# First edge stage of a four-layer graph network: gathered rows held raw in 25 slots, 28 steps ahead

## The reference, cut to what matters

```
edge_index = jnp.stack([src, dst])
# layer 0
row, col = (edge_index[0], edge_index[1])          # row = src, col = dst
msg = x[col] * edge_embed                          # 25000 x 256
agg = segment_sum(msg, row, num_segments=50000)
h   = (1.0 + eps) * x + agg
...
# layer 1 sums edge_attr_64 by src, and counts the edges of each src
sums   = segment_sum(edge_attr_64, src, 50000)
counts = segment_sum(ones, src, 50000)
```

## Time and profile before

| | |
|---|---|
| median of 3 runs | 5857.48 us (5853.29 to 5872.1) |
| the profiled execution, first to last instruction | 5904.5 us |
| PE, DVE, ACT, POOL busy over the span | 73%, 63%, 33%, 61% |
| first phase in that execution | 0 to about 787 us |

### The profile page before, as it was taken

One profiled execution on the slowest core, in us unless ns is written; L12 is line 12 of the kernel. 1 busy time (PEld: TensorE's weight loads), 2 busy tenths in 40 slices (PEclk: granted clock), 3 DMA queues, 4 the chain that ended last, 5 costly groups with the idle time before them and its releaser, 6 DMA issues. The chain is left out here.

```text
span 5904.5 us, 70632 instructions
## 1 busy us (share of the span) xinstructions
PE 4295.0 (73%) x16758; PEld 2844.4 (48%) x16758; DVE 3708.1 (63%) x10195; ACT 1973.8 (33%) x3345; POOL 3605.2 (61%) x3312
## 2 busy tenths in 40 slices
PE   7355569989999999999999777766777400016665
PEld 5243335556666666666666566655666300002222
DVE  6233346656665666666666466668888555458888
ACT  1010135532222222222222122217777300016666
POOL 4388744433556655555555566655777666658787
PEclk9677779999999999999999878778999755559899
DMA  9977789974433333333333233338999522239998
GB/s 368 296 138 137 130 254 365 365 296 161 142 118 120 118 125 118 117 118 118 118 118 114 77 119 120 121 101 300 336 327 320 188 84 82 84 107 344 334 350 305
DMA packets 499110, 1129.62 MB, mean 191 GB/s; under 512 B 165942, under 2 KB 248842, under 8 KB 498966
## 3 DMA queue, kind: packets, MB, share of 16 engines
q1 hardware_dynamic: 333466, 866.21, 42.1%
q0 software_dynamic: 113184, 174.84, 12.5%
q10 hardware_dynamic: 52316, 87.06, 4.2%
HBM read 627.40 MB, written 543.83 MB: 198 GB/s over the span
## 5 line engine op out<-in xcount | busy, mean ns | idle before, releaser
L991 PE MATMUL psum<-arena,W1b 128*128 128x512 f32 x1568 | 727.5, 607 | 0.0
L1014 PE MATMUL psum<-W2b,arena 128*128 128x256 f32 x3136 | 725.5, 379 | 1.9 <-DVE arena L947 1.9
L746 DVE TENSOR_SCALAR arena<-arena 128x256 f32<-128x256 f32 x784 | 462.4, 651 | 365.8 <-POOL arena L741 334.7
L1014 PEld LDWEIGHTS psum<-W2b,arena 128*128 128x128 f32 x3136 | 573.1, 190 | 68.9 <-issue 3.0
L1708 PE MATMUL psum<-arena,ident 128*128 128x512 f32 x784 | 409.1, 671 | 212.2 <-POOL arena L1766 209.9
L904 ACT ACTIVATE arena<-psum,hbias 128x512 f32<-128x512 f32 x392 | 269.2, 687 | 859.0 <-PE psum L991 834.3
L1139 POOL DMA_INDIRECT tab<-arena,IDX x392 | 407.8, 1040 | 203.7 <-issue 117.2
L991 PEld LDWEIGHTS psum<-arena,W1b 128*128 128x128 f32 x1568 | 282.5, 190 | 432.0 <-issue 432.0
L737 POOL TENSOR_TENSOR arena<-arena,lneps 128x4 f32<-128x4 f32 x196 | 39.5, 202 | 731.6 <-DVE arena L733 730.8
L1557 POOL DMA_INDIRECT ad_d<-arena,FE x392 | 399.6, 1019 | 121.1 <-issue 115.3
L1198 PE MATMUL psum<-ident,arena 128*128 128x128 f32 x24 | 5.8, 433 | 608.1 <-issue 598.7
(11 more groups left out here) (232 smaller groups left out, 9334.9 us busy)
## 6 DMA issues: line engine op xcount, KB each, us to landing
arena<-tab SPq DMA_DIRECT2D x194, 544.0 KB
arena<-x_d SPq DMA_DIRECT2D x202, 512.0 KB
arena<-in_x SPq DMA_DIRECT2D x194, 512.0 KB
x_d<-arena SPq DMA_DIRECT2D x194, 512.0 KB
tab<-zero SPq DMA_DIRECT2D x132, 486.0 KB
tab<-blank SPq DMA_DIRECT2D x97, 544.0 KB
h_d<-arena SPq DMA_DIRECT2D x97, 528.0 KB
arena<-h_d SPq DMA_DIRECT2D x97, 528.0 KB
```

Source lines behind the costliest of these rows:

```text
L746: v.tensor_scalar(y[:, j, :], r[:, j, :], self.mv[:, j, 0:1], self.rs[:, j:j + 1], ALU.subtract, ALU.mult).then_inc(self.s["y"], 1)
L991: last = pe.matmul(psum[:, BR + c % RING, :], W1b[:, f, c * P:(c + 1) * P], x1T[:, f, :], start=False, stop=(f == FH - 1))
L1014: last = pe.matmul(outB(j), hid[:, c, j * P:(j + 1) * P], W2b[:, c, :], start=(c == 0), stop=(c == KH - 1))
```

## The change

Gathered rows no longer go into `msg`. They wait as they come in 25 slots (`raw`): 19 new ones (`raws`) and 6 in weight buffers that are loaded only in ACT's last 12 steps. DVE multiplies from there into `msg`. `comb` shrinks from 16 steps to 3, `msg` and the edge features from 4 to 3. POOL gathers 28 steps (112 gathers) before the first scatter, and spreads the other 84 over steps 1 to 40. A gather waits for the multiply that frees its slot, not for PE's sum. Gathers report on one semaphore for each group of six steps. The step loops are written out in full.

```diff
-        NX, NC = 4, 16
+        NX, NC, NR, NGR, GRP = 3, 3, 19, 6, 6
+        UNROLLED = NX * NC * ES
...
+        raws = take([NR, J, D])
+        flat = lambda a: a.rearrange("p f d -> p (f d)")
+        borrowed = [[flat(W1b[:, :, :]), 0], [flat(W2b[:, :, :]), 0], [lent, 0],
+                    [flat(W1a[:, :, :]), flat(W2a[:, :, :])], [W1e[:, :], W1u[:, :]],
+                    [flat(Wg[2][:, :, :]), flat(Wg[3][:, :, :])]]
+        NSLOT = NR + len(borrowed)
+
+        def raw(s, j):
+
+            if NR <= s < NSLOT:
+                one, two = borrowed[s - NR]
+                a, c = (one, j) if isinstance(two, int) else ((one, j) if j < J // 2 else (two, j - J // 2))
+                return a[:, c * D:(c + 1) * D]
+            return raws[:, s if s < NR else (s - NSLOT) % NR, j, :]
...
-        e1_xg = [sem(f"e1_xg{b}") for b in range(NX)]
+        e1_xg = [sem(f"e1_rows{b}") for b in range(NGR)]
+
+        def rows_in(s):
+
+            g = s // GRP
+            return e1_xg[g % NGR], 16 * J * sum(min(GRP, ES - GRP * h) for h in range(g % NGR, g + 1, NGR))
...
@@ p1_scalar, and the same in p1_vector and p1_tensor
-            run_beats(act, ES, body, NC, peel=NC)
+            for s in range(ES):
+                body(beat(s, UNROLLED))
...
@@ p1_gpsimd
-                if j == 0:
-                    wait(pool, q["csum"], J * (s - NX + 1))
-                pool.indirect_dma_start(out=msg[:, s % NX, j, 0:D], out_offset=None, in_=x[:, :],
-                                        in_offset=bass.IndirectOffsetOnAxis(ap=dstI[:, s, j:j + 1], axis=0)).then_inc(e1_xg[s % NX], 16)
+                if j == 0 and s >= NSLOT:
+                    before = s - NSLOT if s < NSLOT + NR else s - NR
+                    pool.wait_ge(q["msg"], J * (before + 1))
+                pool.indirect_dma_start(out=raw(s, j), out_offset=None, in_=x[:, :],
+                                        in_offset=bass.IndirectOffsetOnAxis(ap=dstI[:, s, j:j + 1], axis=0)).then_inc(rows_in(s)[0], 16)
...
-            pool.wait_ge(q["ones"], 1)
-            first = J * (NC + NX + 1)
+            first = J * (NSLOT + 3)
...
-                due = min(J * ES, first - (-(J * ES - first) * max(0, s - 2) // (ES - 7)))
+                due = min(J * ES, first - (-(J * ES - first) * s // (ES - 9)))
...
@@ p1_vector
-                v.wait_ge(e1_xg[k.slot(NX)], 16 * J * (k.turn(NX) + 1))
+                v.wait_ge(*rows_in(k.s))
...
-                    v.tensor_tensor(out=msg[:, k.slot(NX), j, 0:D], in0=msg[:, k.slot(NX), j, 0:D], in1=eat[:, k.slot(NX), j, :], op=ALU.mult).then_inc(q["msg"], 1)
+                    v.tensor_tensor(out=msg[:, k.slot(NX), j, 0:D], in0=raw(k.s, j), in1=eat[:, k.slot(NX), j, :], op=ALU.mult).then_inc(q["msg"], 1)
```

More of the change, by code:

```diff
@@ L269, in gnn_program @@
                  ("idx", "pad", "ones", "srcF", "srow", "same", "cnt", "far", "d", "sidx", "msg",
-                  "csum", "comb", "scat", "prep", "row", "wt")}
+                  "csum", "comb", "scat", "row", "wt")}
         e1_ea = [sem(f"e1_ea{b}") for b in range(NX)]
-        e1_xg = [sem(f"e1_xg{b}") for b in range(NX)]
+        e1_xg = [sem(f"e1_rows{b}") for b in range(NGR)]
+        def rows_in(s):
+            g = s // GRP
+            return e1_xg[g % NGR], 16 * J * sum(min(GRP, ES - GRP * h) for h in range(g % NGR, g + 1, NGR))
         q = edge1
@@ L341, in p1_scalar @@
             for s in range(NX - 1):
-                load(beat(s, NC))
+                load(beat(s, UNROLLED))
             weights = p1_act_loads()
@@ L437, in first @@
                 v.tensor_scalar(srcF[:, k.slot(2), :], srcI[:, k.s, :], 0.0, None, ALU.add).then_inc(q["srcF"], 1)
-            first(beat(0, NC))
+            first(beat(0, UNROLLED))
             def body(k):
@@ L461, in body @@
                 v.tensor_tensor(out=sidx[:, k.s, :], in0=fsd, in1=trash4[:, :], op=ALU.add).then_inc(q["sidx"], 1)
-                v.wait_ge(e1_xg[k.slot(NX)], 16 * J * (k.turn(NX) + 1))
+                v.wait_ge(*rows_in(k.s))
                 v.wait_ge(e1_ea[k.slot(NX)], 32 * (k.turn(NX) + 1))
                 for j in range(J):
-                    v.tensor_tensor(out=msg[:, k.slot(NX), j, 0:D], in0=msg[:, k.slot(NX), j, 0:D], in1=eat[:, k.slot(NX), j, :], op=ALU.mult).then_inc(q["msg"], 1)
-            run_beats(v, ES, body, NC, peel=NC)
+                    v.tensor_tensor(out=msg[:, k.slot(NX), j, 0:D], in0=raw(k.s, j), in1=eat[:, k.slot(NX), j, :], op=ALU.mult).then_inc(q["msg"], 1)
+            for s in range(ES):
+                body(beat(s, UNROLLED))
             v.wait_ge(s_c["w"], nloads[0])
@@ L536, in rows @@
                 last.then_inc(q["srow"], 1)
-            rows(beat(0, NC))
+            rows(beat(0, UNROLLED))
             def body(k):
@@ L548, in body @@
                     last.then_inc(q["csum"], 1)
-            run_beats(pe, ES, body, NC, peel=NC)
+            for s in range(ES):
+                body(beat(s, UNROLLED))
             pe.wait_ge(q["comb"], J * ES)
```

## The result

The changed kernel takes 5892.62 us (median of 5, 5888.51 to 5904.44) against 5857.48 us: ratio 1.0056, interval 1.0041 to 1.0070. It is 35 us slower; 33 us faster was forecast. The profiled execution took 5888.5 us, with a span of 5886.8. Its span is shorter than that of the profiled execution of before (5904.5), which lay 47 us above its median; the two spans are therefore no comparison, but the place where the first phase ends is. DVE's first add of phase two starts at 794.59 us before and at 822.93 us after: 28 us later. No row places the other 7 of the 35 us.

What follows compares the result with a forecast made beforehand. The first edge stage was taken as two stretches in series: the DMA-bound fill, then POOL's list of scatters and gathers. Gains of 18 and 15 us, 33 in all, took 5857.5 to 5824.5 us; range 5803 to 5846.

Steps and rivals of the forecast that it cites:

- Fewer edge loads in the fill: Fill stretch before the first scatter: 6 steps' edge loads instead of 20, first scatter 18 us sooner, bounds 0 and 27.
- More gathers before the first scatter: POOL's scatter stretch: 84 gathers left over 48 periods, undisturbed sum 494.2 us, a cut of 29.0 us.
- Late landings: Scatter periods 35 to 46: all 12 weight-load batches delay landings, 24 us in all, bounds 10 and 29.
- The moved work: PE, DVE and ACT steps moved beside the scatters stay hidden: 8.83 us a step against POOL's 10.2.
- rival 3: Scatter stretch: landings later in all periods, priced at 1 us on each of 36, giving 5860 us; chance 0.07.
- rival 4: First edge stage: PE, DVE and ACT in series set the pace, 15.8 us a step, 160 slower, 6017 us; chance 0.04.
- DVE against POOL: Scatter stretch: 13 more multiplies beside scatters cost 1 us, bound 4; by the skill's exclusion rule 19 us.
- The order at the end: End of the first edge stage: DVE's set-up of the weights stays hidden behind the last scatters, by 8.6 us.
- Rival 2: Fill stretch: it does not end sooner, since 112 gathers in a row keep their queue largest; gain 15, 5842 us; chance 0.08.
- The range: Whole kernel: from 5803 us (gain 54) up to 5846 us (gain 11).
- rival 1: Scatter stretch: late landings no worse than now, stretch 509 us, gain 42, kernel 5815 us; chance 0.23.

Runs made afterwards that it cites:

- e3_lead21: The changed kernel with 84 gathers instead of 112 before the first scatter, still back to back: 5936 us against 5906 for the kernel before, one execution.
- e5_split: The changed kernel with a POOL memset behind each lead gather and the 127- and 106-partition loads cut in two: 5819.35 us against 5867.13 before, ratio 0.9920.
- e1_sp_paced: The changed kernel with POOL's lead gathers paced by SP's count of issued fill transfers: 5865.85 us against 5906.35 before, ratio 0.9923.

## Why the prediction was wrong

Point by point, by its own steps:

- *Fewer edge loads in the fill: wrong, and this alone turned the sign.* The step added up DMA work, 218 us, and held that "the full share says that nothing idles". The sum itself is right: where the gathers leave the others alone, the first scatter comes at 221.98, 222.55 and 222.84 us. What failed is that the DMA engines would be fed. The share was full in a kernel whose gathers PE held back in 16 pieces, 61.2 us of waits; I read those waits as a cost to be removed, and they were what kept POOL below the pace at which the others are held up: 84 gathers from 11.9 to 178.1 us were one per 2.0 us, and the change made it one per 1.25 (e3_lead21 has 84 at that pace, and is held up). The lower bound of the step, a gain of 0, was no bound: nothing excluded a loss.
- The trace of before had rows that fit this, though they show it less plainly. At the end of its only run of 16 gathers in a row, ACT's next copy and POOL's next gather come 4.52 and 3.28 us after their last, although PE had ended by 32.99 us the sums that both waited for; both go on at about 35 us, and by the 1.39 us of above the 16 gathers would be served at 34.1 (an estimate). PE itself did not pause.

```profile
25.12 7.87 PE L546 MATMUL psum<-arena,NEG 128*128 128x324 f32 x20 [9.44 <-issue]
...
30.86 0.95 POOL L398 DMA_INDIRECT arena<-in_x,arena  x1 [0.30 <-issue]
...
34.72 0.44 ACT L359 ACTIVATE arena<-psum 128x324 f32<-128x324 f32 x1 [4.52 <-remote]
35.09 0.95 POOL L398 DMA_INDIRECT arena<-in_x,arena  x1 [3.28 <-remote]
```

- *More gathers before the first scatter: right.* The lead was issued in one run of 1.25 us each (139.3 us for 111), and in the scatter stretch stand 36 periods with two gathers, 4 with three, 8 with none. Undisturbed periods with two took 10.13 to 10.36 us (10.23 forecast).
- *Late landings: right in size, wrong in kind.* Waits are long in nine of periods 35 to 44. Against 494.2 us undisturbed the stretch took 513.9, so the late landings cost about 20 us; I took 24. But the batches are not late alike: nine of the twelve are, and by e5_split the loads of 106 and 127 partitions account for 12 of the 20 us.
- *The moved work: right.* ACT is released by landings, and DVE no longer waits for gathered rows in the scatter stretch. From 240 to 784 us:

```profile
ACT arena L380 <- DMA tab<-arena: 544.4, 46, 125.3
...
POOL tab L432 <- DMA tab<-arena: 36.8, 20, 9.0
```

  Period 5 carries as much DMA work as the fullest one of before at its length (share 0.85 over 10.29 us; 0.87 over 10.20 in the earlier trace rows), and waits 0.45 us; rival 3 did not happen, nor did rival 4 in the scatter stretch.
- *DVE against POOL: right.* A scatter takes 1566 ns in the median and 1847 at most, against 1567 and 1863 before, and the undisturbed periods with two gathers are no longer than forecast (10.21 us in the mean). The 19 us that the prediction works out by the rule of exclusion do not appear.
- *The order at the end: right.* DVE's set-up ran from 780.25 to 802.4 us, and so ended 6.6 us before the last scatter was issued at 809.0:

```profile
780.25 1.69 DVE L504 MEMSET NEG<- 128x1960 f32 x1 [2.33 <-PE psum L569]
...
802.38 0.07 DVE L546 MEMSET bias<- 128x8 f32 x1
```

- *Rival 2* named the right stretch ("112 gathers in a row keep their queue at its largest") with the wrong price, 0 instead of +50 us. With the hold-up removed the change gives what was meant: e1_sp_paced brings the add 41 us forward, and the runs 45 us (0.77%, 0.60% to 0.94%); 33 were forecast.
- *The range* has a slip of its own. Its upper end names the late bound of 29 us and a fill gain of 10, which together are a gain of 20 us and not 11; its lower end, rival 1 with the late bound of 10 or with the fill's bound of 27, is a gain of 47 or 51 and not 54. The measured time lies above either form of it, by the first bullet alone.

## What to carry to other kernels

A wait that paces an engine can be worth having: before you remove one, ask at what pace the engine will run then, and whether the trace has any stretch in which it ran at that pace for as long. A resource that is full now is shown full only as it is fed now; take a work sum as the time only if every feeder can still issue. Where others wait for scatters to land, look for loads beside them whose partition count is not a multiple of 16: cutting those of 106 and 127 partitions took 12 us off the stage.

## What the runs showed of the hardware

- With gathers of 128 rows issued by POOL every 1.25 us for 112 in a row, the transfers, instructions and semaphores of the other engines come late; 48 fill transfers in 90 us fall to 13. At 1.33 us a gather (1.39 with POOL's own waits) it is 25, at 1.445 us 53. With a quarter of the bytes it is 13 again, with half the rows, at 1.22 us, 59.
- The hold-up outlasts the last gather by more the longer the run is: 12 us after 84 gathers and 17 after 112; about 4 us after 16 fit it.
- A load of 106 partitions (424 KB) issued beside scatters delayed their landing from 2.9 to 9.0 us; cut into 96 and 10 it left the landing at 2.87 us.
